# Two-layer adaLN transformer on one core: layer 1's first operands prepared 12 steps sooner, inverse roots and FP4 products moved between DVE and POOL

## The reference, cut to what matters

```python
def exterior(p1, p2):
    L = p1[..., _PI] * p2[..., _PJ] - p1[..., _PJ] * p2[..., _PI]
    n = jnp.clip(jnp.linalg.norm(L, axis=-1, keepdims=True), 1e-12)
    return L / n
...
scale = jnp.max(jnp.abs(xb), axis=-1, keepdims=True) / 6.0      # fp4_quant_dequant, blocks of 16
q = _GRID[idx] * jnp.sign(xn) * scale
...
logits = std_logits + incidence * weights * bias_scale          # incidence from the lines
```

## Time and profile before

| | us |
|---|---|
| median of 3 runs | 1036.51 (1032.13 to 1037.96) |
| the profiled execution, its own time | 1033.47 |
| its span, first to last instruction | 1032.2 |
| busy: PE, DVE, ACT, POOL | 856.5, 742.6, 655.6, 405.4 |
| gate between the layers: last add of layer 0 ends at | 324.55 |
| heads of layer 1 | 326 to 842 |

### The profile page before, as it was taken

One profiled execution on the slowest core, in us unless ns is written; L12 is line 12 of the kernel. 1 busy time (PEld: TensorE's weight loads), 2 busy tenths in 40 slices (PEclk: granted clock), 3 DMA queues, 4 the chain that ended last, 5 costly groups with the idle time before them and its releaser, 6 DMA issues.

```text
span 1032.2 us, 25478 instructions
## 1 busy us (share of the span) xinstructions
PE 856.5 (83%) x9999; PEld 530.8 (51%) x9999; DVE 742.6 (72%) x1783; ACT 655.6 (64%) x1154; POOL 405.4 (39%) x664
## 2 busy tenths in 40 slices
PE   5688788876565698998989899898888868898987
PEld 2344455554433465665656566575565533444434
DVE  4776888898665868777686877868777557666554
ACT  4668888746234275766667575666656747685866
POOL 3043555455866535373543645454132210101000
PEclk8899999998866599999999999999999989999999
DMA  5000000000324252443525334262542000000000
GB/s 149 22 0 1 1 1 0 1 1 1 105 62 121 68 152 69 116 128 80 148 63 140 86 97 122 68 178 47 143 133 66 3 1 1 22 2 21 1 22 21
DMA packets 70698, 63.60 MB, mean 62 GB/s; under 512 B 30600, under 2 KB 62824, under 8 KB 70576
## 3 DMA queue, kind: packets, MB, share of 16 engines
q1 hardware_dynamic: 70064, 61.90, 22.7%
q10 hardware_dynamic: 512, 0.02, 0.0%
HBM read 34.02 MB, written 27.36 MB: 59 GB/s over the span
## 4 chain that ended last, share of the span: by engine, by line
PE 44%; DVE 11%; issue 5%; ACT 5%; POOL 1%; SPq 1%; DMA 1%; DVEq 0%; POOLq 0%; ACTq 0%
PE bank L2082 12%; PE bank L1660 7%; PE bank L1635 3%; PE bank L1608 3%; PE bank L1616 3%; PE bank L1597 2%; PE bank L1590 2%; DVE bank L1744 2%; PE bank L1600 2%; ACT 4g L2140 1%; PE bank L1668 1%; PE bank L1626 1%; DVE 4f L2176 1%; PE bank L1623 1%; DVE roots L1299 1%
## 5 line engine op out<-in xcount | busy, mean ns | idle before, releaser
L1824 ACT ACTIVATE ET<-bank 64x512 f32<-64x512 f32 x128 | 75.3, 589 | 100.3 <-PE bank L1626 99.5
L2163 DVE TENSOR_TENSOR act<-4f,act 128x512 f16<-128x512 f32 x96 | 66.4, 691 | 56.1 <-ACT act L2130 55.9
L1819 ACT ACTIVATE ET<-bank 128x768 f32<-128x768 f32 x128 | 103.1, 805 | 2.4
L1744 DVE TENSOR_TENSOR bank<-bank,W 128x256 f32<-128x256 f32 x128 | 54.7, 427 | 52.6 <-PE bank L1590 52.6
L1660 PE MATMUL bank<-ET,vv 128*32 128x128 f32 (+2 forms) x1792 | 90.0, 326 | 0.8 <-DVE O L1779 0.8
L1754 DVE TENSOR_REDUCE mo<-bank 128x4 f32<-128x512 f32 x128 | 87.3, 682 | 1.6 <-PE bank L1600 1.4
L1749 DVE TENSOR_TENSOR bank<-bank,WT 128x256 f32<-128x256 f32 x128 | 55.1, 430 | 46.1 <-PE bank L1616 43.2
L2130 ACT ACTIVATE act<-4f 128x512 f16<-128x512 f32 x96 | 60.4, 630 | 28.3 <-DVE 4f L2176 26.2
L1762 DVE TENSOR_REDUCE mo<-bank 128x3 f32<-128x384 f32 x128 | 70.0, 547 | 0.0
L1763 DVE TENSOR_REDUCE mo<-bank 128x3 f32<-128x384 f32 x128 | 69.9, 546 | 0.0
L2082 PE MATMUL bank<-act,std 128*128 128x512 f16 x256 | 57.0, 383 | 0.1
(11 more groups left out here) (376 smaller groups left out, 2542.1 us busy)
## 6 DMA issues: line engine op xcount, KB each, us to landing
ring<-scr_q SPq DMA_DIRECT2D x16, 324.0 KB
QO<-scr_q SPq DMA_DIRECT2D x16, 324.0 KB
ring<-scr_a SPq DMA_DIRECT2D x16, 252.0 KB
KA<-scr_a SPq DMA_DIRECT2D x16, 252.0 KB
ring<-scr_k SPq DMA_DIRECT2D x16, 168.0 KB
KB<-scr_k SPq DMA_DIRECT2D x16, 168.0 KB
scr_a<-dk SPq DMA_DIRECT2D x8, 288.0 KB, 2.6
X<-in_x SPq DMA_DIRECT2D x8, 256.0 KB, 5.2
```

Of the source, the lines that this page charges most:

```text
L1744: dve.tensor_tensor(half(psD, 1), half(psD, 1), over(W[:, h * HB:(h + 1) * HB], NT), ALU.mult).then_inc(s_wq, 1)
L1819: act.activation(ET[n % NE][:, T:SEG * P], psXT[:, 0:NP * P], ACT.Exp).then_inc(s_expo, 1)
L1824: act.activation(to[0:HB, :], psDT[0:HB, :], ACT.Exp)
L2163: dve.tensor_tensor(lo, f32_[f % 3], hi, ALU.subtract).then_inc(s_lo, 1)
```

## The change

1. The steps of layer 1's operands begin at slot 147 instead of 159 and come at every second slot, instead of two in three; POOL's come one slot sooner than DVE's and ACT's. Their last step stays at slot 199 (198 before). The waits for the attention's last add move to the steps that write what it reads, 12 steps in; the output weights of attention 0 lie in `dqn` instead of `3xh`, which is written earlier now.
2. For batch 0 DVE does the Newton rounds and the scaling of L. For batches 1 to 7 POOL does, as before.
3. For batches 1 to 7 POOL sums the squares in three adds (384, 128 and 128 columns); DVE's reduction of 768 columns stays for batch 0 alone.
4. For halves x = 11 to 15 DVE does the product with the scales.

```diff
+    BY_DVE = 11
...
     def half_dve(x):
         yield from quantise_dve(dve, half(x), 2 * FF // 16, tmps_b[x % 2], s_hstep, x, [(s_prod, 2 * x + 2)], (s_hq, x - 1) if x >= 2 else ())
+        if x >= BY_DVE:
+            quantise_pool(dve, hq[x % 2], 2 * FF // 16, tmps_b[x % 2], s_hstep, x, s_hq, (s_turn, 2 * (x - 1)))
...
     def half_pool(x):
         yield from blank(9)
-        quantise_pool(pool, hq[x % 2], ...)
+        if x < BY_DVE:
+            quantise_pool(pool, hq[x % 2], ...)
...
-    FREE = 159
+    BEGIN, FREE = 147, 159
+    LINES = 12
     def operands_slot(f, behind):
-        q, r = divmod(f - FREE - behind, 3)
-        n = 2 * q + r - ahead.slots
-        return n if r < 2 and -ahead.slots <= n < 0 else None
+        q, r = divmod(f - BEGIN - behind, 2)
+        return q - ahead.slots if r == 0 and 0 <= q < ahead.slots else None
...
     def operands_dve(b):
-        dve.wait_ge(s_sq, b + 1)
-        dve.tensor_reduce(n2..., sq..., AX.X, ALU.add).then_inc(s_n2, 1)
+        if b == 0:
+            dve.wait_ge(s_sq, 1)
+            dve.tensor_reduce(n2..., sq..., AX.X, ALU.add).then_inc(s_n2, 1)
         dve.wait_ge(s_n2, 2 * b + 1)
...
+        if b == 0:
+            dve.wait_ge(s_rn, 1)
+            yield from newton(dve, b)
...
     def operands_pool(b):
         pool.tensor_tensor(sq, L, L, ALU.mult).then_inc(s_sq, 1)
-        yield from blank(2)
-        pool.wait_ge(s_rn, b + 1)
-        (12 Newton instructions, then L by rn)
+        yield
+        if b:
+            sv, three = sq.rearrange("p (s i h) -> p s i h", s=8, i=NL), NL // 2
+            pool.wait_ge(s_sq, 3 * b - 1)
+            pool.tensor_tensor(sv[:, :, 0:three], sv[:, :, 0:three], sv[:, :, three:NL], ALU.add).then_inc(s_sq, 1)
+            pool.wait_ge(s_sq, 3 * b)
+            pool.tensor_tensor(sv[:, :, 0], sv[:, :, 0], sv[:, :, 1], ALU.add).then_inc(s_sq, 1)
+            pool.wait_ge(s_sq, 3 * b + 1)
+            pool.tensor_tensor(n2..., sv[:, :, 0], sv[:, :, 2], ALU.add).then_inc(s_n2, 1)
+        yield
+        if b:
+            pool.wait_ge(s_rn, b + 1)
+            yield from newton(pool, b)
+        else:
+            yield
```

More of the change, by code:

```diff
@@ L616, in attention0 @@
     first.s_x, first.s_rest, first.s_chans, first.s_rows = s_x, s_rest, s_chans, s_rows
-    first.pe, first.dve, first.act, first.pool, first.s_add, first.signals = on_pe, on_dve, on_act, on_pool, s_add, signals
+    first.pe, first.dve, first.act, first.pool, first.signals = on_pe, on_dve, on_act, on_pool, signals
+    first.s_v, first.s_proj, first.s_add = s_v, s_proj, s_add
     return first
@@ L917, in half_pool @@
         yield from blank(9)
[L918 removed]
+        if x < BY_DVE:
+            quantise_pool(pool, hq[x % 2], 2 * FF // 16, tmps_b[x % 2], s_hstep, x, s_hq, (s_turn, 2 * (x - 1)) if x >= 2 else ())
         if x % 2:
@@ L971, in slot_pe @@
         if n == -ahead.slots:
-            pe.wait_ge(first.s_add, B)
+            pe.wait_ge(first.s_v, B)
         if n is not None:
@@ L977, in slot_dve @@
         n = operands_slot(f, 1)
+        if n in (-ahead.slots, H - ahead.slots):
+            dve.wait_ge(second.s_add, (n + ahead.slots) // H + 1)
         if n is not None:
[L979 to L982, removed]
             ahead.dve(n)
@@ L986, in slot_act @@
         n = operands_slot(f, 1)
-        if n == -ahead.slots:
+        if n == LINES - ahead.slots:
             act.wait_ge(first.s_add, B)
@@ L995, in slot_pool @@
     def slot_pool(f):
-        n = operands_slot(f, 1)
-        if n == -ahead.slots:
+        n = operands_slot(f, 0)
+        if n == LINES - ahead.slots:
             pool.wait_ge(first.s_add, B)
@@ L1105, in attention1 @@
     units = dk_[0:3, 0:G * KX // 2]
-    first_weights = roots, xh[:, 0:D], c.sb("bq", 2, at=held), s_w0
+    first_weights = roots, dqn_.bitcast(F32)[:, 0:D], c.sb("bq", 2, at=held), s_w0
     first_room = raw_.bitcast(F32)[:, 0:T], raw_.bitcast(F32)[:, T:2 * T], L[:, 0:T], sq[:, 0:T]
@@ L1372, in operands_act, with newton @@
             yield
+    def newton(eng, b):
+        for i in range(3):
+            for k, (x_, y_) in enumerate(((rn, rn), (nh, n2))):
+                eng.tensor_tensor(nh, x_, y_, ALU.mult).then_inc(s_newton, 1)
+                eng.wait_ge(s_newton, 12 * b + 4 * i + k + 1)
+            eng.tensor_scalar(nh, nh, -0.5, 1.5, ALU.mult, ALU.add).then_inc(s_newton, 1)
+            eng.wait_ge(s_newton, 12 * b + 4 * i + 3)
+            eng.tensor_tensor(rn, rn, nh, ALU.mult).then_inc(s_newton, 1)
+            eng.wait_ge(s_newton, 12 * b + 4 * i + 4)
+            if i == 1:
+                yield
+        Lv = L.rearrange("p (s i h) -> p s i h", s=8, i=NL)
+        eng.tensor_tensor(Lv, Lv, rn.rearrange("p (s o h) -> p s o h", s=8, o=1).to_broadcast([P, 8, NL, H]), ALU.mult).then_inc(s_Ln, 1)
     def operands_pool(b):
@@ L1421, in operands_pool @@
         pool.tensor_tensor(sq, L, L, ALU.mult).then_inc(s_sq, 1)
-        yield from blank(2)
-        pool.wait_ge(s_rn, b + 1)
[L1424 to L1434, removed]
+        yield
+        if b:
[5 more added lines that the diff above has]
+            pool.wait_ge(s_sq, 3 * b + 1)
+            pool.tensor_tensor(n2.rearrange("p (s h) -> p s h", s=8), sv[:, :, 0], sv[:, :, 2], ALU.add).then_inc(s_n2, 1)
+        yield
+        if b:
+            pool.wait_ge(s_rn, b + 1)
+            yield from newton(pool, b)
+        else:
+            yield
         yield from blank(4)
```

3 lines of the change are left out of this document (1 added, 2 removed).

## The result

The changed kernel takes 1029.18 us, median of 7 runs (1027.37 to 1031.47), against 1036.51 (1032.13 to 1039.23) of the kernel before: ratio 0.9939, interval 0.9914 to 0.9964, so 0.6% faster. The forecast was 1026.5 in a range from 1019 to 1035. Timed once more, the same kernel gave 1028.95 and a ratio of 0.9931 (0.9910 to 0.9952). The profiled execution took 1027.37, its span is 1026.1.

A forecast was written before the change was run, and what follows sets the result against it. No engine was taken as full late in layer 0: hand-overs bound it. 7.2 + 1.3 = 8.5 us off the profiled 1033.5 gave 1025.0, and from the mean of 1035.0 the forecast was 1026.5, range 1019 to 1035.

The forecast's parts named there:

- Operands sooner: Late in layer 0: products begin 8.1 us sooner, near 256.4; 10.1 us from there to sq, ready at 266.5.
- the lock: POOL and certain DVE instructions exclude each other for a whole instruction; 1 us counted as lost late in layer 0.
- Reduction and Newton on DVE: Late in layer 0: DVE's reduction, Newton rounds and scaling give L at 277.9 instead of 287.18, 9.3 us sooner.
- From L to the end: Late in layer 0: second raw 291.1, 2Y of batch 6 296.8, last hand-over 6.4, end 317.3, 7.2 us sooner.
- SP: End of layer 0: SP's DMA issuing is late next, ending at 314.8 to 316.9, under the layer's end at 317.3.
- The adds: Heads, batches 1 to 7: POOL's three adds take 2.05 us against DVE's 1.44; 1.3 us gained in sum.
- batch 2: Heads: DVE waits for POOL's adds until 395.68 instead of 395.02, 0.7 us lost.
- The sum: Whole kernel: 7.2 us from layer 0 and 1.3 from the heads, 8.5 us off.
- lock eats the front: Rival, layer 0: lag of 4 and locked DVE instructions leave 2 us of the 7.2; 1032 us; chance 0.13.
- adds late: Rival, heads: adds of 3.6 us lose near 10, 1036 us; at 2.8 they lose 4, 1032; chance 0.11.
- last xq: Rival, late in layer 0: batch 7's xq, 3.2 us later, sets the end; 1042 us at worst; chance 0.10.
- The base of 1035.0: Whole kernel before: mean of all four executions shown, 1035.0 us, from which the forecast of 1026.5 was taken.

The follow-up runs named there:

- e7: Changed kernel with the operands' steps of layer 1's first batch back at their old places, the other parts kept; 1030.38 us, ratio 0.9942.
- e5: Changed kernel with the first batch's Newton steps and scaling of the lines on POOL again; 1029.67 us, ratio 0.9945.
- the fair pair: Second executions, without any edit, of the kernel before (1037.07 us) and the changed kernel (1028.95 us), both with the first drop to half clock.
- e10: Changed kernel with batch 2's squares reduced by VectorE and, from batch 3, POOL's squares to scaled lines in one piece, X add behind; 1021.72 us, ratio 0.9866.

## Why the prediction was right, point by point

- **Operands sooner.** The products were forecast for 256.4 and sq for 266.5; they came at 254.13 and 267.41. The start was 2.3 sooner than forecast, and the 10.1 us from there to sq were mis-sized: 13.28, in every trace with all front parts, against 10.93 with the old places (e7). Single instructions of POOL took up to twice their time there (0.90 for 0.45). That VectorE's held them, the lock from its other side, is argued; the forecast had nothing for it. The waits shrank as said. The places alone are worth 2.8 us of the front (e7).
- **Reduction and Newton on DVE.** L scaled at 279.09, forecast 277.9. Right in time, wrong in what it bought: with POOL it would have been 279.20 (e5). The 2.65 us of this part come later: 0.9 by the last hq of VectorE, and 1.75 behind it from PE's clock, of which one trace can't say whether it belongs to the part.
- **From L to the end.** Second raw 293.2 (291.1 forecast), 2Y of batch 6 at 299.72 (296.8), end 317.30 (317.3). The last hit rests on two errors that cancel, which is luck: 2Y of batch 6 came 2.9 later than forecast, VectorE's stretch behind it took from 299.72 to 310.75 + 1.16 = 311.91, 12.2 against the 12.1 forecast, and the last hand-over 3.35 in place of 6.4. The forecast took 0.5 off the 6.90 for the product; the hand-over became 3.55 shorter, 1.75 by PE's full clock and 1.8 because VectorE's own stretch ends with hq now, where PE used to wait for POOL's behind it. Two offsets between the two traces cancel as well: the changed kernel's starts 1.65 sooner, and it has the drop near 250 us that the kernel before as shown has not. In the fair pair the front gain is 7.2, forecast 7.2.
- **SP.** Its last DMA instruction (313.73, 1.43 us) ends at 315.16, forecast 314.8 to 316.9. It did not bind.
- **The adds.** 2.07 us against 2.05; batch 1 +1.3 (1.3 forecast), five batches +0.15 each (0.14). **The term that was mis-sized is batch 2**: 0.7 forecast, 2.0 in five traces of seven, because PE drops to half clock behind the wait. Without this the sum of the heads is +1.3, with it 0.
- **The sum.** 8.5 forecast. The medians differ by 7.3, and 7.2 + 0 is what the paired traces give. The rivals (lock eats the front, adds late, last xq) did not happen. The lock did cost more than the 1 us counted: on POOL's way to sq, if I put it down to that, 3.2, and on VectorE 1.83 for 0.88 once and three of the five hq products at 1.16 to 1.83. The Newton instructions and the scaling of L on VectorE were not held (0.22 to 0.30, and 0.96). How much of this reached the end no run separates.
- The base of 1035.0, the mean of four runs, was 0.4 to 2.1 us too low: more runs put the kernel before at 1035.4 to 1037.1. The difference of 2.7 to 1026.5 is this and batch 2.
- Two figures beside the sum do not follow from their terms. Adds of 2.9 us in place of 2.05 would turn the +1.3 of the heads into a loss of 4.6; the 6 is the distance between the two, and 0.7 a batch holds for batches 3 to 7 alone. And adds of 3.6, with the front gain of 7.2 kept, give some 1037, not 1036. Neither enters the forecast, and the adds took 2.07.

Open is why a drop comes in one execution and not in the next; and whether e5's late loss comes with the part or was chance, for which one execution is too few.

## What to carry to other kernels

A wait that vanishes is not a gain until one has asked what next waits on the same chain, and by how little it does not wait yet. Here the start value of the root, asked for one step later, lost its wait of 1.2 us; the rounds and the scaling behind it had 0.15 us to spare, and PE waited 2.6 for them instead. What paid was to keep that step where it was and to take the foreign add of 1.27 us out from in front of it (e10). A wait that stays the same whatever comes before it, as the 0.76 here, is not one for that chain: read whether the engine in between was idle. And profile the unaltered kernel twice before explaining a difference of 2 us between two traces.

## What was not expected of the hardware

Two executions of one program differ by stretches at half clock in one place and full clock in the other: 1.7 us each in layer 0, 1.3 in the heads, 3.4 us in sum at the first head. PE went to half clock behind an idle stretch of 1.97 us in batch 2 in five executions of seven, and not behind those of 1.1 us in batches 3 to 7 of the kernel after. And a lock between VectorE and POOL can be as long as the wait that it replaces: 1.27 for an instruction of 0.23.
